# A new order for the first batch of a masked attention with residual and layer norm, in fp32 by split products

## The reference

```python
q = einsum('bnd,ed->bne', x, Wq); k = einsum('bnd,ed->bne', x, Wk); v = einsum('bnd,ed->bne', x, Wv)
rel = einsum('bnd,bmd->bnm', q, k)              # 16 x 1024 x 1024
rel = adj.T[None] * rel                         # a 0/1 mask, the same for all batches
rel = rel / norm(rel, axis=2, keepdims=True)
out = layernorm(x + einsum('bnm,bmd->bnd', rel, v), eps=1e-5)
```

## Time and profile before

| | |
|---|---|
| median of 3 runs | 1971.75 us (1971.14 to 1971.92) |
| the profiled execution | 1971.97 us, span 1970.2 us |
| TensorE busy | 1957.0 us, 99% of the span |
| VectorE busy | 1531.9 us, 78% |
| GpSimd busy | 957.8 us, 49% |
| ScalarE busy | 762.5 us, 39% |
| chain that ended last | TensorE 97%, VectorE 1%, GpSimd 1% |

### The profile page before, as it was taken

How to read it: one execution, slowest core, us unless ns; L and a number is a source line. 1 busy time by engine, 2 the same in 40 slices (tenths; PEclk the granted TensorE clock), 3 DMA queues, 4 the chain that set the end, 5 groups by cost and what they waited for, 6 DMA issues and landing times.

```text
span 1970.2 us, 28685 instructions
## 1 busy us (share of the span) xinstructions
PE 1957.0 (99%) x9857; PEld 1669.1 (85%) x9857; DVE 1531.9 (78%) x2085; ACT 762.5 (39%) x1288; POOL 957.8 (49%) x639
## 2 busy tenths in 40 slices
PE   8999999999999999999999999999999999999998
PEld 6888888888888888888888888888888888888887
DVE  8796877868778696787968779687796877868775
ACT  5433434335342352423424234342433424335341
POOL 5744536455354553446435374453644536455352
PEclk9999999999999999999999999999999999999999
DMA  5734343344524345343444333443434343344401
GB/s 188 314 134 165 144 167 115 144 154 154 186 92 149 142 157 184 122 151 118 157 175 160 128 139 133 172 153 128 160 128 170 144 155 127 144 154 152 185 26 64
DMA packets 80416, 292.22 MB, mean 148 GB/s; under 512 B 7441, under 2 KB 7441, under 8 KB 76305
## 3 DMA queue, kind: packets, MB, share of 16 engines
q1 hardware_dynamic: 80400, 292.06, 40.2%
HBM read 251.13 MB, written 40.89 MB: 148 GB/s over the span
## 4 chain that ended last, share of the span: by engine, by line
PE 97%; DVE 1%; POOL 1%; DMA 0%; issue 0%; SPq 0%; ACT 0%; POOLq 0%; DVEq 0%
PE banks L422 32%; PE banks L424 32%; PE banks L423 32%; DMA scr<-xT 0%; DVE aw L794 0%; DVE x_lo L755 0%; POOL scr L1063 0%; DVE yv L816 0%; POOL square_sum L1067 0%; POOL squares L1067 0%; SPq L344 0%; POOL scr L1072 0%; SPq L343 0%; POOL res L1075 0%; POOL res L1080 0%
## 5 line engine op out<-in xcount | busy, mean ns | idle before, releaser
L422 PE MATMUL banks<-yv 128*128 128x512 f32 x1024 | 399.8, 390 | 0.0
L424 PE MATMUL banks<-yv 128*128 128x512 f32 x1024 | 398.5, 389 | 0.0
L423 PE MATMUL banks<-yv 128*128 128x512 f32 x1024 | 398.5, 389 | 0.0
L1119 POOL TENSOR_TENSOR square_sum<-square_sum,squares 128x512 f32<-128x512 f32 x224 | 319.9, 1428 | 85.7 <-ACT squares L657 75.1
L422 PE MATMUL banks<-yv,x_hi 128*128 128x512 f32 x896 | 348.7, 389 | 0.5 <-DVE rel L857 0.5
L424 PE MATMUL banks<-yv,x_lo 128*128 128x512 f32 x896 | 348.6, 389 | 0.0
L423 PE MATMUL banks<-yv,x_hi 128*128 128x512 f32 x896 | 348.6, 389 | 0.0
L1136 POOL TENSOR_TENSOR rstd<-var_eps,minus_half 128x1 f32<-128x1 f32 x128 | 144.2, 1127 | 329.3 <-DVE var_eps L968 329.3
L423 PE MATMUL banks<-aw,x_hi 128*128 128x256 f32 x896 | 253.6, 283 | 0.0
L424 PE MATMUL banks<-aw,x_lo 128*128 128x256 f32 x896 | 253.5, 283 | 0.0
L422 PE MATMUL banks<-aw,x_hi 128*128 128x256 f32 x896 | 253.5, 283 | 0.0
(11 more groups left out here) (108 smaller groups left out, 3430.5 us busy)
## 6 DMA issues: line engine op xcount, KB each, us to landing
scr<-adj SPq DMA_DIRECT2D x128, 512.0 KB, 5.8
aw<-w_kept SPq DMA_DIRECT2D x16, 3584.0 KB, 11.1
aw<-a_kept SPq DMA_DIRECT2D x15, 3584.0 KB, 11.0
scr<-xT SPq DMA_DIRECT2D x32, 1024.0 KB, 7.1
res<-x SPq DMA_DIRECT2D x128, 256.0 KB, 2.7
out<-res SPq DMA_DIRECT2D x128, 256.0 KB, 2.0
a_kept<-aw SPq DMA_DIRECT2D x1, 3584.0 KB, 18.2
w_kept<-v_raw SPq DMA_DIRECT2D x3, 512.0 KB, 8.5
```

The source lines that it names most:

```text
L422: pe.matmul(bank_ap, l_hi, r_hi, start=first and i == 0, stop=False, skip_group_check=on)
L423: pe.matmul(bank_ap, l_hi, r_lo, start=False, stop=False, skip_group_check=on)
L424: mm = pe.matmul(bank_ap, l_lo, r_hi, start=False, stop=i == len(pairs) - 1, skip_group_check=on)
L1119: pool.tensor_tensor(square_sum[:, h, :], square_sum[:, h, :], squares[:, n % SQRING, :], ALU.add).then_inc(square_added, 1)
```

## The change

It touches the first batch and what stands ahead of it; in the later batches the pieces of x are made in a new order too (`X_PIECES`, S2 before S3). In short:

- TensorE computes A in an order by what is ready (the high by high products of a row of weights before the low parts exist), the blocks of A's first half before those of the second; the six fill products go.
- x's first half of the rows is loaded first. X11 and B11 are made first; the sums S1 and S2 of x go to free places in `rel`; GpSimd makes S1, S3 and S4 and T3's low part; T3's split has a semaphore of its own.
- Wv's sums T1..T4 go to `v_raw` on GpSimd, behind S4. Its high parts are made by ScalarE behind the fourth square of pair 0, straight into `aw`, its low parts by VectorE in pairs between the score blocks: two behind c21 of pair 0, two behind c12 of pair 0, two behind the first additions of pair 1, the last behind m11 of pair 1.
- SyncE loads mask tiles 2 and 3 early. In the first batch it stores A's pieces, waits for the last of Wv's low parts (`w_loaded`, now an increment by VectorE), stores all of Wv's pieces from `aw` in one DMA, loads the four residual tiles, and then mask tiles 6 and 7. The stores in pieces and the first load of `w_kept` go.

```diff
-X_PIECES = (X22, X11, S1, X12, S3, S2, S4)
+X_PIECES = (X11, X22, S1, X12, S2, S3, S4)
...
+        first_raw_of.update({S1: rel[:, 2:4, BANK:N], S2: rel[:, HT:HT + 2, 0:BANK]})
...
         def wv_sum_block(i):
-            return scr[:, adj_slot[2], i * BANK:(i + 1) * BANK].rearrange("p (d e) -> p d e", d=2)
+            return v_raw[:, i, :].rearrange("p (d e) -> p d e", d=2)
...
-        A_PIECES = (B11, T1, B21, T2, T4, T3, B22)
+        A_PIECES = (B11, T1, B21, T2, T4, B22)
...
-            load_x(0)
+            load_x(0, (0, 1))
...
+            load_adj(2)
             load_adj(3)
-            for i in range(3):
-                store_wv(i)
...
                 if first:
-                    for i in range(3, 7):
-                        store_wv(i)
-                    load_adj(2)
-                    sp.wait_ge(a_split, 7)
+                    sp.wait_ge(a_split, len(A_PIECES))
+                    sp.wait_ge(a_t3_split, 1)
                     sp.dma_start(a_kept, aw[:, :].bitcast(F32)).then_inc(a_stored, DMA)
+
+                    sp.wait_ge(w_loaded, DMA)
+                    sp.dma_start(w_kept, aw[:, :].bitcast(F32)).then_inc(w_stored, DMA)
                     for t in range(RRING):
                         load_res(0, t)
-                    for i in range(WSLOTS):
-                        sp.wait_ge(w_stored[i], 2 * DMA if i < 3 else DMA)
-                    sp.wait_ge(a_stored, DMA)
-
-                sp.wait_ge(y_done, b * Y_COUNT + Y_COUNT)
-                sp.dma_start(aw[:, :].bitcast(F32), w_kept).then_inc(w_loaded, DMA)
+                else:
+                    sp.wait_ge(y_done, b * Y_COUNT + Y_COUNT)
+                    sp.dma_start(aw[:, :].bitcast(F32), w_kept).then_inc(w_loaded, DMA)
                 sp.wait_ge(s_m12, b * HT + 1)
                 load_adj(6)
...
+            for ks, js in (((0, 1), range(KD)), ((2, 3), (0, 1)), ((2, 3), (2, 3))):
+                for k in ks:
+                    pe.wait_ge(w_hi_made, 2 * k + 2)
+                    for j in js:
+                        pe.matmul(bank[A_BANK + j], wq_hi[:, k, cols(j)], wk_hi[:, k, :], ...)
+                    pe.wait_ge(w_split, 2 * k + 1)
+                    for j in js:
+                        pe.matmul(bank[A_BANK + j], wq_lo[:, k, cols(j)], wk_hi[:, k, :], ...)
+                    pe.wait_ge(w_split, 2 * k + 2)
+                    for j in js:
+                        mm = pe.matmul(bank[A_BANK + j], wq_hi[:, k, cols(j)], wk_lo[:, k, :], ...)
...
# ScalarE, ahead of the batch
-            for q in (X22, X11, S1):
-                x_piece(0, q, True)
+            x_piece(0, X11, True)
             a_hi_piece(B11)
             act.activation(a12_raw, a_block(0, 1), ACT.Copy).then_inc(a12_copied, 1)
-            for q in (B21, B22, T1):
+            x_piece(0, X22, True)
+            a_hi_piece(T1)
+            x_piece(0, S1, True)
+            x_piece(0, X12, True)
+            for q in (B21, B22):
                 a_hi_piece(q)
...
# ScalarE, in the first batch's y_blocks
-                    for i in range(3, 7):
-                        wv_hi_piece(i)
+                    a_hi_piece(T4)
+                    a_hi_piece(T3)
+                    x_piece(b, S3, True)
+                    x_piece(b, S4, True)
...
# ScalarE, wv_hi_piece
+                act.wait_ge(a_stored, DMA)
+                act.wait_ge(y_done, Y_COUNT)
+                act.activation(wv_hi[:, q, :, :], wv_raw_of[q], ACT.Copy).then_inc(wv_hi_made, 1)
...
+                for name, i in square_order[0:4]:
+                    square(b, name, i)
                 if first:
-                    for i in range(WSLOTS):
-                        act.wait_ge(w_stored[i], 2 * DMA if i < 3 else DMA)
-                for name, i in square_order[0:6]:
+                    for i in range(7):
+                        wv_hi_piece(i)
+                for name, i in square_order[4:6]:
                     square(b, name, i)
...
# VectorE
+            x_piece(0, X11, True)
             a_lo_piece(B11)
             a_sum_of(T1)
+            x_piece(0, X22, True)
             a_lo_piece(T1)
+            x_piece(0, S1, True)
+            dve.wait_ge(first_sum[S1], 1)
+            dve.tensor_tensor(first_raw_of[S2], first_raw_of[S1], raw_of[X11], ...)
+            x_piece(0, X12, True)
+            a_lo_piece(B21)
+            a_sum_of(T2)
+            x_piece(0, S2, True)
+            a_lo_piece(T2)
             a_sum_of(T3)
             a_sum_of(T4)
+
+            def wv_lo_piece(i):
+                q = WV_PIECES[i]
+                dve.wait_ge(wv_hi_made, i + 1)
+                lo = dve.tensor_tensor(wv_lo[:, q, :, :], wv_raw_of[q], wv_hi[:, q, :, :].bitcast(F32), ALU.subtract)
+                if i == 6:
+                    lo.then_inc(w_loaded, DMA)
...
# VectorE, y_blocks of the first batch, behind the two additions of round 6
+                    x_piece(b, S3, True)
+                    for j in range(2):
+                        y_lo_piece(b, B11, j, a[j])
+                    x_piece(b, S4, True)
+                    a_lo_piece(B22)
...
# GpSimd
+            pool.wait_ge(x_loaded[1], DMA)
+            pool.tensor_tensor(first_raw_of[S1], x21_raw, raw_of[X22], ALU.add).then_inc(first_sum[S1], 1)
             pool.wait_ge(first_sum[S1], 1)
-            pool.wait_ge(x_loaded[0], DMA)
-            pool.wait_ge(a_split, 1)
+            pool.wait_ge(a_split, a_place[T2])
             pool.tensor_tensor(raw_of[S3], raw_of[X11], x21_raw, ALU.subtract).then_inc(first_sum[S3], 1)
+            pool.wait_ge(a_hi_made, a_hi_place[T3])
+            pool.tensor_tensor(a_lo[:, T3, :, :], a_raw_of[T3], a_hi[:, T3, :, :].bitcast(F32), ...)
             pool.wait_ge(first_sum[S2], 1)
+            pool.tensor_tensor(raw_of[S4], raw_of[X12], first_raw_of[S2], ALU.subtract).then_inc(first_sum[S4], 1)
+            for q in WV_SUMS:
+                wv_sum_of(q)
```

More of the change, by code:

```diff
@@ L97, in adjacency_attention_layernorm @@
         a_stored = sem("a_stored")
-        w_stored = [sem(f"w_stored{i}") for i in range(WSLOTS)]
+        w_stored = sem("w_stored")
         a_loaded = sem("a_loaded")
@@ L315, in adjacency_attention_layernorm @@
                     T1: a_sum_block(0), T2: a_sum_block(1), T3: a_sum_block(2), T4: a_sum_block(3)}
-        A_PIECES = (B11, T1, B21, T2, T4, T3, B22)
-        A_SUMS = (T1, T3, T2, T4)
-        A_HI = (B11, B21, B22, T1, T2, T4, T3)
+        A_PIECES = (B11, T1, B21, T2, T4, B22)
+        A_SUMS = (T1, T2, T3, T4)
+        A_HI = (B11, T1, B21, B22, T2, T4, T3)
         a_place = {q: i + 1 for i, q in enumerate(A_PIECES)}
@@ L332, in load_adj, with load_x @@
                 sp.dma_start(scr[:, adj_slot[m], :], adj_v[:, m, :]).then_inc(adj_loaded[m], DMA)
-            def load_x(b):
-                for n in (1, 0):
+            def load_x(b, halves=(1, 0)):
+                for n in halves:
                     rows = slice(n * BANK, (n + 1) * BANK)
@@ L395, in batch @@
                     sp.wait_ge(v_done, b * V_COUNT + V_COUNT)
+                    if first:
+                        sp.wait_ge(a_stored, DMA)
+                        sp.wait_ge(w_stored, DMA)
                     sp.dma_start(aw[:, :].bitcast(F32), a_kept).then_inc(a_loaded, DMA)
@@ L738, in _ @@
             y_first(0)
-            x_piece(0, S3, True)
             x_piece(0, S2, True)
[L741 to L745, removed]
+            a_hi_piece(T2)
             batch(0, True, False)
@@ L752, in _, with x_piece @@
         def _(dve):
[L753 removed]
+            def x_piece(b, q, first=False):
+                raw = first_raw_of[q] if first else raw_of[q]
                 dve.wait_ge(x_hi_made, b * 7 + x_place[q])
[L755 removed]
+                dve.tensor_tensor(x_lo[:, q, :, :], raw, x_hi[:, q, :, :].bitcast(F32),
                                   ALU.subtract).then_inc(x_split, 1)
@@ L828, in y_blocks @@
                 a, bb, c = y_bank["a"], y_bank["b"], y_bank["c"]
[L829 to L833, removed]
+                if not first:
+                    for j in range(2):
+                        y_lo_piece(b, B11, j, a[j])
                 for j in range(2):
@@ L839, in y_blocks @@
                 if first:
-                    x_piece(0, S4)
+                    x_piece(b, S3, True)
+                    for j in range(2):
+                        y_lo_piece(b, B11, j, a[j])
+                    x_piece(b, S4, True)
+                    a_lo_piece(B22)
+                    dve.wait_ge(a_split, len(A_PIECES))
+                    dve.wait_ge(a_t3_split, 1)
                 for j in range(2):
@@ L859, in y_blocks, with s_blocks @@
                     y_lo_piece(b, B21, j, y_b21_raw[j])
-            def s_blocks(b, pair):
+            def s_blocks(b, pair, first):
                 a, bb, c = (s_bank[pair][n] for n in ("a", "b", "c"))
@@ L868, in s_blocks @@
                     dve.tensor_tensor(c12(i), c[i % 2], c21(i), ALU.add).then_inc(s_u2, 1)
```

(32 more changed lines are left out.)

98 lines of the change are left out of this document (28 added, 70 removed).

## The result

The changed kernel took 1980.87 us (median of 6 runs, 1979.75 to 1981.67), the kernel before 1971.84 beside it: a ratio of 1.0045, 95% interval 1.0035 to 1.0056. It is 9.0 us slower; forecast were 1981 and 9.1. The profiled execution took 1981.49 us, its span is 1979.7 (before 1970.2).

A forecast was written before the change was run, and what follows sets the result against it. TensorE, 99% busy, was taken as the bound. V's round 2 moving from 90.96 to 97.5 (+6.5) plus slow clock (+2.6) took 1971.97 to 1981.1, stated as 1981, range 1977.5 to 1984 (chance 0.65).

The forecast's parts named there:

- What bounds it: Whole kernel: TensorE, 99% busy, sets the time; after 49.63 us its shifts reach the end unless a new wait arises.
- The front end: First batch up to the scores: work from VectorE's round 7 additions on runs 7.2 to 7.4 us earlier, taken as 7.3.
- The idle products' end at 5.31: Start of TensorE's work: A can start at 5.31 instead of 6.00 us, ending near 16.4 instead of 17.24.
- the 1.47 us of fill products lay on the path, and go: Between A and Y's round 1: removing the fill products was counted as saving 1.47 us on the path.
- The wait of 1.1 us forecast at round 5: Y's round 5 in the first batch: TensorE waits 1.1 us for S1 and T1, then runs 20.2 to 23.1.
- The turns of VectorE and GpSimd: With VectorE inputs in SBUF and GpSimd working, each waits for the other's whole instruction; two x_lo pieces took 5.61, not 2.4 us.
- The queue: SyncE's DMAs after w_loaded: store 11 us, residuals 2.7, tile 1.3, so mask tile 6 lands at 87.6 us.
- Rival 1: Mask tiles do not queue behind the store: tile 6 lands at 81.6, total 1975 us; chance 0.10.
- The chain from tile to copy: Masks and squares from tile 6 to ScalarE's v_copy(0) take 9.9 us, so V's round 2 starts at 97.5.
- The slow clock: After TensorE's 13 us stand at V's round 2: clock at 0.50 for some 6 us, costing 2.6 us.
- I charge no slow clock: Y's waits of 1.1 and 2.0 us in the front are too short to lower the clock; 2.9 us if wrong.
- Rival 2: The new wait at V hides and the front's 7.3 us reach the end: 1964.7 us; chance 0.11.

The follow-up runs named there:

- with the tiles first: Changed kernel with mask tiles 6 and 7 issued ahead of the wait for w_loaded, the store of Wv's pieces and the residual loads: 1965.75 us, ratio 0.9968.
- with nothing but the store in front: Changed kernel with only the four residual loads moved behind mask tiles 6 and 7, the store staying ahead: 1978.76 us, ratio 1.0034.
- the order wait, tiles, store: Changed kernel with mask tiles 6 and 7 right behind the wait for w_loaded, ahead of the store and residual loads: 1968.71 us, ratio 0.9982.
- three other orders of the front: Kernel issuing mask tiles before that wait, plus: B22's low part before S4's, 1965.79 us; S4's sum on VectorE, 1966.09; that with GpSimd's Wv sums held back, 1966.21.
- S4 on VectorE: Kernel issuing mask tiles before the w_loaded wait, with S4's sum moved from GpSimd to VectorE and B22's low part ahead of S4's: 1966.09 us.
- copies first: Changed kernel with ScalarE's two copies of V's round 1 ahead of pair 1's m22, m21 and m12 squares, first batch: 1980.18 us, ratio 1.0041.

## Why the prediction was right, and which of its errors offset each other

**What bounds it.** TensorE saturated from 49.6 us on, shifts passing to the end one for one: held. 9.4 of 9.5 us are accounted for at V's round 2. The trace of the kernel before has one wait more than the prediction lists, 0.51 us for VectorE at 19.21; the sum does not use it, since the front is timed by VectorE's chain.

**The front end.** Gain 7.3 forecast, 6.9 measured (round 6 at 42.3, measured 42.70). Two steps in it were off. The idle products' end at 5.31 was read from one execution; in this one the eleven idle products and A's first four matmuls ran at 0.43 to 0.48 us each, about the pace after 32.42 with the clock at 0.50 (14 steps in 6.07 us), and Y's round 1 started at 17.58 in place of 16.4. The granted clock reads 1.00 there; why the pace was low is open. And "the 1.47 us of fill products lay on the path, and go" was wrong, by the prediction's own next lines: round 5 hangs on S1's chain (20.2 forecast, 20.55 measured), so TensorE waits there for whatever it saves before. The run with the fill products put back shows it. The wait of 1.1 us forecast at round 5 was there in other profiles (1.58 with the tiles first) and in this one swallowed by the late A (0.25 us left).

**The turns of VectorE and GpSimd** carried every time after 15 us. S4's sum took 3.45 us, 2.3 plus the 1.1 of one VectorE piece; round 3 was forecast at 36.1 and started at 36.55; the store of Wv's pieces was forecast at 72.6 and issued at 72.58.

**The queue.** The step that made the forecast. Tile 6 was put at 87.6 and the masks began at 89.11. The large transfer was put at 11 us to landing and took 11.0; the residuals were put at 2.7 us and cost 2.7. The term that was too small is the tile's own, 1.3 us: with nothing but the store in front its mask starts 2.8 us after the store has landed, so the 1.5 us are there without the residuals, and the 4.0 us that SyncE takes to issue these don't explain them. Rival 1, with the Trainium skill's rule behind it (DMA: Bandwidth & Descriptors, "Two DMAs through the same engine are not ordered"), asked for a landing near 81.6; the masks' starts at 76.8, 86.2 and 89.1 say no for a store of this size. That does not contradict the Trainium skill, which has the descriptors of one queue start in order and lets a later one finish while an earlier one still writes. Whether single descriptors of the tile finished early no view here shows.

**The chain from tile to copy** was put at 9.9 us and took 9.2 (89.1 to 98.3). This error offsets half of that of the landing, so round 2 came at 98.3 for 97.5.

**The slow clock** was put at 2.6 us after this wait and cost 2.1. With it the 0.8 us of round 2 shrink to 0.3: 9.4 us for the forecast 9.1. That the medians differ by 9.0 is closer than the steps deserve, and in part luck. "I charge no slow clock" for the front's waits held for the changed kernel (1.81 us), and was nearer to failing than I wrote: waits of 2.27 and 1.89 us in variants brought it down.

**Rival 2** (the gain reaches the end) described the kernel with the tiles first: 1964.7 for it, 1965.75 measured. Its condition, tiles landing before 74 to 78 us, was the right place to look: in the order wait, tiles, store the mask starts at 76.8, and the time lies between, at 1968.71.

## What to carry to other kernels

When a store is gathered into one large transfer and waits for its last piece, list what stands behind it in the queue: a small load that was early becomes late by the wait and by every byte in front, here 12.0 us of bytes and 5.5 of waiting (the tiles issued at 72.26 in place of 66.80). Price the transfer by its landing in the trace, and look for an order in which the loads that somebody waits for go first; here it cost a few moved lines and was worth 15 us. Before crediting a saving, find the next thing that the engine waits for: here 1.47 us of removed products and three other orders of the front, meant to be better, brought nothing.

## What the runs showed of the hardware that I had not expected

In these profiles the clock's fall can't be told from the length of an idle time alone. It stayed whole through the first 2.8 us of idleness in the earlier trace rows and through 1.8 us at round 3 in the kernel with the tiles first, but fell behind waits of 2.27 us (S4 on VectorE), 2.0 us (wait, tiles, store) and 1.89 us (copies first; TensorE was back at full clock for some 3 us there after a longer stop). The moment differs too: in the first two of these the granted clock goes down 0.1 to 0.2 us before the matmuls begin again (at 36.7 and 86.3 us), in the third 1.5 us after they have (at 108.2). What decides was not settled.
